# A two-stage mixture of experts on one core: later loads of the two split matrices, their means in a shared product, and the place of the expert's register load

## What is computed

```python
# x: 4 x 512 tokens of 512 numbers; itok: a token id for each; ctx: 4 matrices of 512 x 512
h = layernorm(x)
e1 = minimum(clip(itok, 0, 24999) // 6250, 3)          # expert of the first stage
x = x + ((silu(h @ ctx[e1].T) * (h @ ctx[e1].T)) @ ctx[e1].T)
h = layernorm(x)
e2 = argmax(h @ router_w.T)                            # one of 8 experts
# every product below is a bitlinear: weights to -1, 0, 1 by their mean absolute value,
# activations to 8 bits by the row's largest absolute value
x = x + bitlinear(square(relu(bitlinear(h, wg[e2]))) * bitlinear(h, wu[e2]), wd[e2])
```

## Time and profile before

| | us |
|---|---|
| median of 3 runs | 289.84 (289.49 to 291.39) |
| the profiled execution | 291.08 |
| its span in the profile | 289.3 |
| TensorE busy | 249.7 (86%) |
| VectorE busy | 222.3 (77%) |
| ScalarE busy | 213.4 (74%) |
| GpSimd busy | 153.7 (53%) |

### The profile page before, as it was taken

One profiled execution on the slowest core, in us unless ns is written; L12 is line 12 of the kernel. 1 busy time (PEld: TensorE's weight loads), 2 busy tenths in 40 slices (PEclk: granted clock), 3 DMA queues, 4 the chain that ended last, 5 costly groups with the idle time before them and its releaser, 6 DMA issues.

```text
span 289.3 us, 5775 instructions
## 1 busy us (share of the span) xinstructions
PE 249.7 (86%) x1425; PEld 179.5 (62%) x1435; DVE 222.3 (77%) x662; ACT 213.4 (74%) x322; POOL 153.7 (53%) x277
## 2 busy tenths in 40 slices
PE   2168889999999998799999999896698989999880
PEld 2135668888888887588888888762244444444440
DVE  5868897888868872877877778888968778878771
ACT  2778677989878884678888887765467878878770
POOL 3434015665556563545636642577565576575744
PEclk9997799999999999599999999999779999999996
DMA  6998357566535639346645544340476883101110
GB/s 227 432 361 321 122 184 318 174 212 209 186 110 202 200 127 395 98 165 218 208 145 175 186 168 182 114 148 8 127 285 221 278 267 117 73 35 61 57 37 0
DMA packets 13839, 51.72 MB, mean 179 GB/s; under 512 B 2862, under 2 KB 2862, under 8 KB 10224
## 3 DMA queue, kind: packets, MB, share of 16 engines
q1 hardware_dynamic: 8928, 37.91, 37.3%
q0 software_dynamic: 4880, 13.44, 13.4%
HBM read 40.49 MB, written 13.48 MB: 187 GB/s over the span
## 4 chain that ended last, share of the span: by engine, by line
PE 73%; DVE 9%; issue 7%; ACT 4%; DMA 4%; POOL 2%; SPq 0%; DVEq 0%; POOLq 0%
PE bank L1276 35%; PE bank L1386 19%; PE bank L1269 8%; PE bank L1358 5%; PE bank L1380 3%; DMA staged<-weight_chunks 3%; ACT ternary L535 1%; PE bank L1292 1%; POOL x L405 1%; POOL out_rows L498 1%; DVE fac L1097 1%; DVE ternary L749 1%; DVE prod L1087 1%; PE bank L1463 1%; DMA token_ids<-token_ids_in 1%
## 5 line engine op out<-in xcount | busy, mean ns | idle before, releaser
L1386 PE MATMUL bank<-ternary,qT 128*128 x179 | 45.2, 393 | 4.0 <-issue 3.4
L535 ACT ACTIVATE ternary<-staged 128x2048 bf16<-128x2048 f32 x22 | 42.0, 1910 | 5.1 <-DMA staged<-weight_chunks 5.1
L541 ACT ACTIVATE ternary<-staged,w_scale 128x1536 int16<-128x1536 f32 x22 | 34.5, 1566 | 2.6 <-DVE w_scale L793 2.3
L1386 PEld LDWEIGHTS bank<-ternary,qT 128*128 128x128 bf16 x184 | 18.3, 100 | 28.4 <-issue 14.9
L405 POOL DMA_INDIRECT x<-x_rows,gather x19 | 20.9, 1101 | 18.9 <-DVE row L881 15.7
L444 POOL DMA_INDIRECT x_rows<-row,store_at x19 | 21.9, 1155 | 16.7 <-POOL store_at L440 14.4
L498 POOL DMA_INDIRECT out_rows<-late_rows x18 | 19.1, 1061 | 14.9 <-DVE late_rows L1116 12.2
L415 POOL TENSOR_TENSOR rstd<-var_eps,half_powers 128x1 f32<-128x1 f32 x19 | 13.3, 700 | 24.7 <-DVE var_eps L839 24.3
L1386 PE MATMUL bank<-ternary,rT 128*128 x87 | 23.5, 390 | 2.9 <-DVE late_rows L1116 1.4
L618 ACT ACTIVATE relu<-bank 128x512 f32<-128x512 f32 x23 | 13.8, 598 | 15.4 <-PE bank L1386 14.7
L862 DVE TENSOR_TENSOR p<-bank,p 128x512 f32<-128x512 f32 x19 | 13.1, 691 | 15.1 <-ACT p L584 15.1
(11 more groups left out here) (214 smaller groups left out, 662.2 us busy)
## 6 DMA issues: line engine op xcount, KB each, us to landing
staged<-weight_chunks SPq DMA_DIRECT2D x22, 1024.0 KB
late_rows<-x_rows SPq DMA_DIRECT2D x18, 260.0 KB, 3.2
ternary<-ctx_chunks SPq DMA_DIRECT2D x4, 1024.0 KB, 8.9
x_rows<-filler SPq DMA_DIRECT2D x9, 260.0 KB
ternary<-weight_chunks SPq DMA_DIRECT2D x2, 1024.0 KB, 4.8
staged<-x_rows SPq DMA_DIRECT2D x5, 260.0 KB, 3.5
x<-x_rows,gather POOLq DMA_INDIRECT x19, 3.5
x_rows<-row,store_at POOLq DMA_INDIRECT x19
```

Source lines behind the costliest of these rows:

```text
L535: nc.scalar.activation(ternary[:, m * K * D:(m + 1) * K * D], staged[i % 2][:, :], ACT.Abs, accum_out=abs_sum[:, m:m + 1]).then_inc(abs_re ...
L541: nc.scalar.activation(ternary[:, m * K * D + DVE_COLS:(m + 1) * K * D].bitcast(I16), staged[i % 2][:, DVE_COLS:], ACT.Copy, scale=w_scale ...
L1386: last = pe.matmul(ps[:, :], left[:, k * P:(k + 1) * P], ternary[:, bass.ds(e * (3 * K * D) + (kind * K + k) * D, D)], start=(k == 0), sto ...
```

## The change

- Other matrices are split: `EXTRA` is (21, 22) instead of (20, 21). `extra` is the storage of ternary matrices 22 and 23, so the second split matrix now ends in the storage in which it was loaded. So its absolute values go to a scratch tile `dump` (line 549 wrote them into `ternary`), and every scale piece waits for the one before.
- The second split matrix starts a tick later (`FIRST_PIECE` (3, 11) instead of (3, 10)), and its load stands behind `load_weights(14)`, not behind `load_weights(12)`.
- The order of ScalarE in a tick: the scale piece stands ahead of `sum_abs`, the sum piece still behind it.
- The sums of a split matrix are added up by VectorE (`extra_total`) into the column of `abs_sum` next to that of the whole matrix of the following tick, and `sum_mean` takes both columns in one product. `sum_extra_mean` is gone. The mean, the scale pieces and the cut come one tick later than before: scale pieces in ticks 8, 9, 10 and 16, 17, 18 (before 7, 8, 9 and 14, 15, 16), cuts in 11 and 19 (before 10 and 17).
- VectorE: `hT_rest(1)` directly behind `gate(0)`.
- TensorE, second stage: `load_ffn_expert(u + 1)` directly behind `up_product(u)`, not at the end of the step.

The diff:

```diff
@@ the plan of the split matrices
-EXTRA = (20, 21)
+EXTRA = (21, 22)
...
-FIRST_PIECE = (3, 10)
+FIRST_PIECE = (3, 11)
 EXTRA_SUMS = {FIRST_PIECE[i] + j: (i, j) for i in range(2) for j in range(SUM_PIECES)}
-EXTRA_MEAN = {FIRST_PIECE[i] + SUM_PIECES: i for i in range(2)}
-EXTRA_SCALES = {FIRST_PIECE[i] + SUM_PIECES + j: (i, j) for i in range(2) for j in range(SCALE_PIECES)}
-EXTRA_CUT = {FIRST_PIECE[i] + SUM_PIECES + SCALE_PIECES: i for i in range(2)}
+EXTRA_TOTAL = {FIRST_PIECE[i] + SUM_PIECES: i for i in range(2)}
+EXTRA_MEAN = {FIRST_PIECE[i] + SUM_PIECES + 1: i for i in range(2)}
+EXTRA_SCALES = {FIRST_PIECE[i] + SUM_PIECES + 1 + j: (i, j) for i in range(2) for j in range(SCALE_PIECES)}
+EXTRA_CUT = {FIRST_PIECE[i] + SUM_PIECES + 1 + SCALE_PIECES: i for i in range(2)}
@@ SyncE
-                if i == FIRST_PIECE[1] + ABOVE:
+                if i == FIRST_PIECE[1] + ABOVE + 1:
                     sp.wait_ge(extra_part, SCALE_PIECES)
                     sp.dma_start(extra, weights_in[EXTRA[1]]).then_inc(extra_in, 16)
@@ ScalarE
                 nc.scalar.activation(ternary[:, m * K * D:(m + 1) * K * D], staged[i % 2][:, :], ACT.Abs,
-                                     accum_out=abs_sum[:, m:m + 1]).then_inc(abs_ready, 1)
+                                     accum_out=abs_sum[:, 2 * i:2 * i + 1]).then_inc(abs_ready, 1)
...
-                nc.scalar.activation(ternary[:, first:first + n], extra[:, j * n:(j + 1) * n], ACT.Abs,
+                if x or j:
+                    act.wait_ge(extra_abs_ready, SUM_PIECES * x + j)
+                nc.scalar.activation(dump[:, :], extra[:, j * n:(j + 1) * n], ACT.Abs,
...
                 if j == 0:
                     act.wait_ge(extra_abs_ready, SUM_PIECES * (x + 1))
+                else:
+                    act.wait_ge(extra_part, SCALE_PIECES * x + j)
...
                 evict_hT(t + 1)
+                if t in EXTRA_SCALES:
+                    scale_piece(*EXTRA_SCALES[t])
                 sum_abs(t + 1 + ABOVE)
                 if t in EXTRA_SUMS:
                     sum_piece(*EXTRA_SUMS[t])
-                if t in EXTRA_SCALES:
-                    scale_piece(*EXTRA_SCALES[t])
@@ VectorE
+            def extra_total(x, i):
+
+                dve.wait_ge(extra_abs_ready, SUM_PIECES * (x + 1))
+                dve.tensor_reduce(abs_sum[:, 2 * i + 1:2 * i + 2], extra_sum[:, SUM_PIECES * x:SUM_PIECES * (x + 1)],
+                                  X, ALU.add).then_inc(extra_total_ready, 1)
...
             gate(0)
+            hT_rest(1)
             mean_of(2)
             scale_of(2)
             moments_of(2)
-            hT_rest(1)
...
+                if t in EXTRA_TOTAL:
+                    extra_total(EXTRA_TOTAL[t], t + 1 + ABOVE)
                 if t in EXTRA_CUT:
                     extra_cut(EXTRA_CUT[t])
                 cut(t + ABOVE)
@@ TensorE
             def sum_mean(i):
-                m = ORDER[i]
+                t = i - ABOVE
+                n = 2 if t in EXTRA_MEAN else 1
                 pe.wait_ge(abs_ready, i + 1)
+                if n == 2:
+                    pe.wait_ge(extra_total_ready, EXTRA_MEAN[t] + 1)
                 if i >= 1:
                     pe.wait_ge(w_mean_ready, i)
-                pe.matmul(mean_ps[:, 64 + m:65 + m], ones[:, :], abs_sum[:, m:m + 1], start=False,
-                          stop=True, skip_group_check=True).then_inc(mean_ready, 1)
...
+                pe.matmul(mean_ps[:, 64 + 2 * i:64 + 2 * i + n], ones[:, :], abs_sum[:, 2 * i:2 * i + n],
+                          start=False, stop=True, skip_group_check=True).then_inc(mean_ready, 1)
...
                 transpose_p(t - 1)
-                if t in EXTRA_MEAN:
-                    sum_extra_mean(EXTRA_MEAN[t], t + ABOVE)
                 sum_mean(t + ABOVE)
...
                 gate_product(u)
                 up_product(u)
+                load_ffn_expert(u + 1)
                 transpose_q(u + 1)
                 transpose_r(u - 2)
                 down_product(u - 3)
-                load_ffn_expert(u + 1)
```

More of the change, by code:

```diff
@@ L144, in moe_program @@
         router_sum = sb("router_sum", [P, E2], F32)
-        abs_sum = sb("abs_sum", [P, MATS], F32)
+        abs_sum = sb("abs_sum", [P, 2 * len(ORDER)], F32)
+        dump = sb("dump", [P, K * D // SUM_PIECES], BF16)
         extra_sum = sb("extra_sum", [P, 2 * SUM_PIECES], F32)
@@ L218, in moe_program @@
         ctx_raw = [spare(16 + 2 * e, 2 * K * D, F32) for e in range(E1)]
+        assert EXTRA[1] == MATS - 2
         extra = ctx_raw[E1 - 1]
@@ L262, in moe_program @@
         dve_part, act_part, cut_ready = sem("dve_part"), sem("act_part"), sem("cut_ready")
-        extra_in, extra_abs_ready, extra_mean_ready, extra_scale_ready, extra_part = (
-            sem(n) for n in ("extra_in", "extra_abs_ready", "extra_mean_ready", "extra_scale_ready", "extra_part"))
+        extra_in, extra_abs_ready, extra_total_ready, extra_mean_ready, extra_scale_ready, extra_part = (
+            sem(n) for n in ("extra_in", "extra_abs_ready", "extra_total_ready", "extra_mean_ready", "extra_scale_ready",
+                             "extra_part"))
         x_in_sem = [sem(f"x_in{i}") for i in range(RING)]
@@ L546, in sum_piece @@
                 n = K * D // SUM_PIECES
-                first = EXTRA[x] * K * D + j * n
                 act.wait_ge(extra_in, 16 * (x + 1))
-                nc.scalar.activation(ternary[:, first:first + n], extra[:, j * n:(j + 1) * n], ACT.Abs,
+                if x or j:
+                    act.wait_ge(extra_abs_ready, SUM_PIECES * x + j)
+                nc.scalar.activation(dump[:, :], extra[:, j * n:(j + 1) * n], ACT.Abs,
                                      accum_out=extra_sum[:, SUM_PIECES * x + j:SUM_PIECES * x + j + 1])\
@@ L786, in mean_of @@
                 dve.wait_ge(mean_ready, i + 1)
-                dve.tensor_scalar(w_mean[:, m:m + 1], mean_ps[:, 64 + m:65 + m], 1.0 / (D * D), EPS,
+                dve.tensor_scalar(w_mean[:, m:m + 1], mean_ps[:, 64 + 2 * i:65 + 2 * i], 1.0 / (D * D), EPS,
                                   ALU.mult, ALU.max).then_inc(w_mean_ready, 1)
@@ L1164, in _ @@
                 if t in EXTRA_MEAN:
-                    extra_mean(EXTRA_MEAN[t])
+                    extra_mean(EXTRA_MEAN[t], t + ABOVE)
                 next(interlude, None)
@@ L1287, in sum_mean @@
             def sum_mean(i):
-                m = ORDER[i]
+                t = i - ABOVE
+                n = 2 if t in EXTRA_MEAN else 1
                 pe.wait_ge(abs_ready, i + 1)
+                if n == 2:
+                    pe.wait_ge(extra_total_ready, EXTRA_MEAN[t] + 1)
                 if i >= 1:
                     pe.wait_ge(w_mean_ready, i)
-                pe.matmul(mean_ps[:, 64 + m:65 + m], ones[:, :], abs_sum[:, m:m + 1], start=False,
-                          stop=True, skip_group_check=True).then_inc(mean_ready, 1)
-            def sum_extra_mean(x, i):
-                m = EXTRA[x]
-                pe.wait_ge(extra_abs_ready, SUM_PIECES * (x + 1))
-                pe.wait_ge(w_mean_ready, i)
-                for j in range(SUM_PIECES):
-                    col = SUM_PIECES * x + j
-                    pe.matmul(mean_ps[:, 64 + m:65 + m], ones[:, :], extra_sum[:, col:col + 1], start=False,
-                              stop=(j == SUM_PIECES - 1), skip_group_check=True)
+                pe.matmul(mean_ps[:, 64 + 2 * i:64 + 2 * i + n], ones[:, :], abs_sum[:, 2 * i:2 * i + n],
+                          start=False, stop=True, skip_group_check=True).then_inc(mean_ready, 1)
             def transpose_h(b):
```

4 lines of the change are left out of this document (2 added, 2 removed).

## The result

| | us |
|---|---|
| changed kernel, median of 4 runs | 279.67 (279.12 to 280.31) |
| kernel before, beside it, median of 4 runs | 290.62 (289.49 to 291.41) |
| ratio | 0.9627, 95% interval 0.9581 to 0.9673 |
| profiled execution after, and its span | 279.12, 277.3 |

The change makes the kernel 10.95 us faster; the forecast was 278.5. Between the two profiled executions the span got 289.3 - 277.3 = 12.0 us shorter. All of the following is read against these 12.0. In this document medians are over all runs of a kernel, and ratios leave out the slow ones, which took over 1.5% longer than the fastest run of the same kernel.

The account below looks back on a forecast made before the run. TensorE was taken as the bound, with 73% of the chain that ended last. Terms 5.8 + 1.8 + 0.7 - 0.2 + 3.2 = 11.3 us, taken from the 289.84 median, gave 278.5 us; range 276.2 to 282.2.

Parts of the forecast that it names:

- split load, place in the queue: First stage, ticks 9 to 12: second split load behind load 14 removes the DMA stall; 5.82 us gained, bounds 0 and 5.82.
- means in one product: TensorE, two first-stage ticks: a second column replaces the eight small matmuls at no cost; 1.76 us gained.
- hT_rest(1), start of tick 2: VectorE, first ticks: earlier low half lets block 1's gate start earlier; 0.71 us gained, bounds 0 and 0.9.
- last tick: VectorE: last matrix's cut moves to tick 19, ahead of residual(18); 0.2 us lost, bounds 0 and 0.69.
- register load behind the up product: TensorE, second stage: load hidden behind eight matmuls, removing a 0.38 us gap per two steps; 3.2 us gained, bounds 0 and 4.6.
- The rival that the stall moves: First-stage DMA: two close loads still delay gathered rows, giving back 5.8 us, so 284.3 us; chance 0.09.
- Scale pieces at nothing: ScalarE, six ticks: scale pieces ahead of the absolute sum cost nothing; uncovered, up to 0.85 us each, 5.1 in all.
- The rival of the load that sticks out: Second stage: register load 0.3 us longer outlasts the eight matmuls; 2.6 of 3.2 us go, 281.1 us; chance 0.04.
- The slower case: Second stage: load stops TensorE's sequencer ahead of the transposes, 0.7 us in 20 steps, 14.0 lost, 295.7 us; chance 0.02.

Follow-up runs that it names:

- place alone: Kernel before with only the second split load moved behind load 13 instead of ahead of it: 284.82 us, ratio 0.9794.
- means apart: Changed kernel with the split matrix's mean again taken by four matmuls of its own in ticks 8 and 16: 281.97 us, ratio 0.9719.
- the order alone: Kernel before with only the scale pieces put ahead of the absolute sum on ScalarE: 288.08 us, ratio 0.9863 without the two longest runs.
- the register load alone: Kernel before with only the expert's register load moved behind the up product: 286.82 us, ratio 0.9849.
- hT_rest(1) alone: Kernel before with only that VectorE instruction moved directly behind gate(0): 289.61 us, ratio 0.9965.
- load back: Changed kernel with the expert's register load at the end of the step again: 283.58 us, ratio 0.9781.
- load twice: Changed kernel with each second-stage register load from block 3 on made twice in its new place: 287.01 us, ratio 0.9899.

## Why the prediction was right, point by point

The sum was 11.3 and the spans differ by 12.0. That the two are so close is in part luck: hT_rest(1) gave 0.6 us less than its term, the register load 0.7 more, and the ordinary ticks 0.5 that had no term. Where the terms stand:

| term | forecast | profile | shown by |
|---|---|---|---|
| split load, place in the queue | 5.82 | 5.82 | place alone: all of it |
| means in one product | 1.76 | 1.76 | means apart: 0.89 a tick |
| hT_rest(1), start of tick 2 | 0.71 | 0.12 | undone: nothing that can be told |
| last tick | -0.2 | -0.17 | residual at the same place |
| register load behind the up product | 3.2 | 3.89 | alone 3.74, undone 3.9 |
| ordinary ticks | 0 | 0.5 | cause open |

- *Split matrices.* The mechanism and the size held: two loads at once behind a late scale piece. My account gave the place and the order of ScalarE a share in it together. The runs separate them: the place alone removes 5.8, the order alone 4.0 of it, and with the place changed the order adds nothing. The 5.8 is itself no fixed size, since it contains the half clock behind the idle time: the two stalled ticks stand 5.8 us over two ordinary ones in the kernel before, 5.4 with the register load alone, and 4.3 with hT_rest(1) alone, whose queue and order are the same. The rival that the stall moves is refuted by the ticks of 8.03 to 8.06. Gathers still come late (VectorE's statistics wait for them six times between 40 and 181 us, 4.8 us in all, 1.5 at most), but TensorE has no gap from it. How much two close loads do to a gather is seen in the run with the order alone: 7.72 us in its chain, where the changed kernel's page has 3.6 as the median of 19.

```profile
112.12 7.72 DMA x<-x_rows,gather
```

```profile
x<-x_rows,gather POOLq DMA_INDIRECT x19, 3.6
```

  The Trainium skill ("DMA: Bandwidth & Descriptors", "Queues, rings and completion order") lets the queues take turns packet by packet; by these rows a gather is held up all the same, to twice its time.
- *Scale pieces at nothing.* Right: 0.60 us of room is left in tick 8, where 0.5 had been said.
- *Means.* Right: 8.05 for a tick with the product of two columns, 8.94 with the products apart. The two reductions cost nothing.
- *hT_rest(1): this step failed.* I read that "0.71 is what gets through" from the distance of the gates, and that distance did shrink: it is 6.98 or 6.99 us in all nine profiles in which the instruction is early. What I overlooked is why gate(1) had been late. It waited for ScalarE behind a product of 4.62 us, some 1.7 more than at full clock, since TensorE's granted clock was at 0.5 for a stretch there; 1.0 of these 1.7 was hidden behind low_halves(2). Where the stretch doesn't fall there, the early instruction isn't needed: in the profile with the order on ScalarE alone, and hT_rest(1) in its old place, block 0's product was the slow one and the gates were 6.85 apart. And in the profiles with the instruction early the stretch lies elsewhere each time: just ahead of block 0's product or on it in five profiles, the changed kernel's among them, or on block 2's in four (hT_rest alone, means apart, load back, load twice), whose tick then takes 9.5 us with no cover at all. So the first product of tick 3 starts at 48.59 to 49.08 us in the four profiles with the old place and slow block 1, and at 48.40 to 49.69 in the nine with it early. That the move drives the stretch away isn't shown: each kernel has one profile, and the changed kernel and those with the load back or twice are the same program up to there and still have it in different places. The times don't show a gain from the move either: undone, it costs nothing that can be told, and the 1.0 us gained where it is done alone stand in the profile in the stalled ticks, and vanish between runs of the same granted clock.
- *Last tick.* I said that 0.2 of a cut would be left over at residual(18). Nothing is: it starts 12.18 us into the tick both times. The 0.17 that the profile does lose behind it lies in the first steps of the second stage, where TensorE ran at half clock in stretches that differ between the two profiles; how much of it is theirs stays open.
- *Register load.* Right in mechanism; the term was mis-sized, 3.2 for 3.89 in the profile, between the bounds of 0 and 4.6. The loop holds one gap in two steps, as I had it, but the one gap of 0.38 that I read was a small one: behind the late down products of the version with the load back it is 0.44 and 0.60, and 0.46 for two steps over 17 would give the 3.9. The profiles of other kernels with the same second stage have 56.79 to 57.21 for the 17 steps, so 3.0 to 3.9 is what can be said. The rival of the load that sticks out is refuted: 300 ns as before, and 0.26 us lost in 17 steps against no loads at all, which is less than profiles of the same second stage differ by, and some 1 us at most by the times. The Trainium skill ("DMA: Bandwidth & Descriptors", "Latency and other measured facts") gives some 600 ns as the floor of a tensor_load; the trace doesn't agree for this one. But the rival had a sound core: one load leaves 0.2 us of cover, and with two the kernel loses 0.41 us a step (63.3 less 56.29, over 17). The slower case would have been the same mechanism at a larger size.
- *The median.* Forecast 278.5, measured 279.67. The kernel before was measured at 290.62 beside it, 0.78 above the 289.84 from which I had subtracted; the gain itself was 0.35 short of 11.3.

What stays open: ordinary ticks are 0.03 us shorter in the changed kernel, 0.5 over 16 ticks. The kernels built on the changed one all have it, whether the load, hT_rest, the means or the order are undone; those built on the kernel before have none of it. Some 0.02 of it lies in the four matmuls of the low half, 4 ns each, in the grouped lines from 50 to 100 us, first the changed kernel, then the kernel before:

```profile
L1294 PE MATMUL bank<-ctx_hi,hT_lo 128*128 x27 | 7.2, 389 | 0.0
```

```profile
L1276 PE MATMUL bank<-ctx_hi,hT_lo 128*128 x24 | 6.5, 393 | 0.0
```

What is left as a cause is a part that no run undid alone, such as where the tiles lie once `dump` is added. It was not tried.

## What to carry to other kernels

When two bulk loads leave together, ask which instruction holds back the first of them, and whether either is needed at once: here a load cost 5.8 us because of its place in one queue, although its first piece wasn't due until some seven microseconds later (an estimate: the absolute sum of tick 10 could have started 3.93 us before 115.29, and the sum piece stands 1.9 behind it; the load went out at 105.94). A register load on TensorE's sequencer was nearly free here behind matmuls that outlast their own issue (0.216 against 0.12 us each), and that cover is a budget that can be worked out per place (matmuls times the difference, less the load) and tested by doubling the load. And before a gain at a wait is booked, ask whether the waiting time was made by a clock stretch: in another execution that stretch may fall somewhere else, perhaps where nothing hides it.

## What the runs showed that was not expected

- Where TensorE's granted clock falls to 0.5 in the first 50 us decides over 1 us of the time: the first product of tick 3 starts at 48.40 to 49.69 us by it, the one profile with a longer low stretch left out. Its mean over an execution also changes from run to run of one kernel: 0.944 to 0.978 in 17 runs of the kernel before, which took 295.27 to 288.94 us. In the profiles the place of the low stretch goes along with that of hT_rest(1), though no run shows that this is the cause. The granted clock was 0.57 to 0.72 from 30 to 34 us in four profiles with hT_rest(1) in its old place, 1.00 there in the fifth (the order on ScalarE alone), and 1.00 in all nine with it early, which have their low stretch in 22 to 30 us or in 38 to 46 us.
- A register load holds TensorE's sequencer much longer than its own row says: the two loads of the doubled version start 0.8 us apart (242.4 and 243.2), though they last 0.46 and 0.30.
- VectorE's two waits are exchangeable: with the output ahead of quantise the steps were 3.42 us on average, 3.29 to 3.55 each, with quantise ahead in the same step 3.1 and 3.5 in turn. Only moving quantise out of the step shortened both.
